# A 32-batch attention and mixture block on one core: projections cut into 64-row half passes that are played between the scores

## The reference, cut to what matters

```
mod = silu(c) @ wmod                                    # six rows per batch: sa, ca, ga, sb, cb, gb
h   = layernorm(x) * (1 + ca) + sa
q, k, v = split(h @ w_qkv.T + b_qkv)
P   = softmax(q @ k.T / 4 + alibi_and_causal_mask)      # per head, 512 x 512
x   = x + ga * ((P @ v) @ w_out.T + b_out)
h   = layernorm(x) * (1 + cb) + sb
p   = softmax(h @ gate_W.T)                             # 8 experts
cnt = [experts of the token with p > 0.3 counted; only the numbers 0 and 1 weigh]
x   = x + gb * ((cnt-weighted sum over two experts) @ out_W.T)
```

## Time and profile before

| | |
|---|---|
| median of 3 runs | 1565.01 us (1564.07 to 1567.11) |
| span of the profiled execution | 1560.2 us, so the runs lie 3.9 to 6.9 us above it (the profiled execution has no time of its own beside its span) |
| PE busy | 1472.0 us, 94% |
| DVE busy | 1277.9 us, 82% |
| ACT busy | 1147.2 us, 74% |
| POOL busy | 858.0 us, 55% |
| mean granted TensorE clock | 0.983 of full speed |

### The profile page before, as it was taken

The page is one execution under the profiler, slowest core; times in us unless marked ns, Lnnn a source line. Parts: engine busy times, 40 slices in busy tenths (PEclk is TensorE's granted clock), DMA queues, the critical chain, the costliest instruction groups (busy, mean ns, idle before and its releaser), DMA issues.

```text
span 1560.2 us, 56229 instructions
## 1 busy us (share of the span) xinstructions
PE 1472.0 (94%) x21476; PEld 946.3 (61%) x21476; DVE 1277.9 (82%) x3030; ACT 1147.2 (74%) x2464; POOL 858.0 (55%) x924
## 2 busy tenths in 40 slices
PE   6888999999999999999999999999999999999996
PEld 5555656666666666666666666656666656666653
DVE  6777888888888888888888888888888888888836
ACT  2477777778777777777877877777777777777762
POOL 2124556556556556655655665565665565566454
PEclk9799999999999999999999999999999999999988
DMA  5344555555455555455555545555545555554521
GB/s 170 99 150 127 171 156 173 152 170 157 149 178 155 175 153 166 143 168 167 157 180 152 160 146 170 166 160 157 165 142 167 175 150 178 154 169 139 157 73 50
DMA packets 197298, 239.73 MB, mean 154 GB/s; under 512 B 22462, under 2 KB 147782, under 8 KB 197030
## 3 DMA queue, kind: packets, MB, share of 16 engines
q1 hardware_dynamic: 196972, 236.07, 49.4%
q10 hardware_dynamic: 64, 0.07, 0.0%
HBM read 134.25 MB, written 100.73 MB: 151 GB/s over the span
## 4 chain that ended last, share of the span: by engine, by line
PE 62%; DVE 10%; DMA 9%; issue 6%; SPq 6%; ACT 3%; POOL 2%; POOLq 0%; DVEq 0%; ACTq 0%
PE ps L599 26%; PE ps L753 11%; PE ps L748 8%; PE ps L807 6%; DMA qk_d<-qk_st 5%; PE ps L802 5%; DVE mxp L1089 3%; DMA kz<-qk_d 2%; PE ps L768 2%; PE ps L662 2%; SPq L412 2%; DVE ve_c L1014 1%; DVE zr L1101 1%; DVE st_c L1000 1%; SPq L429 1%
## 5 line engine op out<-in xcount | busy, mean ns | idle before, releaser
L1089 DVE TENSOR_REDUCE mxp<-ps 128x4 f32<-128x512 f32 (+1 forms) x1536 | 842.8, 592 | 160.5 <-PE ps L768 155.6
L863 ACT ACTIVATE prob<-ps 128x512 f32<-128x512 f32 (+1 forms) x1536 | 732.6, 525 | 121.8 <-PE ps L753 116.4
L753 PE MATMUL ps<-qs,kz 50*128 50x128 f16 (+2 forms) x3584 | 405.9, 240 | 12.9 <-DVE mxp L1089 10.5
L768 PE MATMUL ps<-kz,qs 49*128 49x128 f16 (+1 forms) x4096 | 410.5, 231 | 0.1
L753 PEld LDWEIGHTS ps<-qs,kz 50*128 50x128 f16 x3584 | 261.4, 94 | 88.7 <-ACT prob L863 31.1
L768 PEld LDWEIGHTS ps<-kz,qs 49*128 49x128 f16 x4096 | 286.3, 95 | 3.8 <-DVE mxp L1089 1.8
L1347 POOL TENSOR_TENSOR om<-oc,rz 128x512 f32<-128x512 f32 x62 | 77.4, 1270 | 329.9 <-DMA rz<-rz_d 329.9
L807 PE MATMUL ps<-prob,va 128*32 128x384 f32 (+2 forms) x3072 | 237.6, 381 | 0.0
L748 PE MATMUL ps<-mk 64*128 64x256 bf16 x1024 | 198.6, 274 | 36.0 <-DMA kz<-qk_d 11.3
L802 PE MATMUL ps<-prob,va 128*32 128x128 f32 x4096 | 209.6, 277 | 0.6 <-DVE qk_st L1021 0.6
L764 PE MATMUL ps<-mk 64*128 64x256 bf16 x1024 | 201.0, 276 | 5.4 <-DVE mxp L1089 3.4
(11 more groups left out here) (157 smaller groups left out, 2870.6 us busy)
## 6 DMA issues: line engine op xcount, KB each, us to landing
qk_d<-qk_st SPq DMA_DIRECT2D x128, 256.0 KB, 2.8
ou_d<-ou SPq DMA_DIRECT2D x124, 256.0 KB, 2.3
qs<-qk_d SPq DMA_DIRECT2D x256, 96.0 KB, 2.4
kz<-qk_d SPq DMA_DIRECT2D x256, 96.0 KB, 2.5
xa<-in_L_attn_x SPq DMA_DIRECT2D x32, 512.0 KB, 5.2
qk_d<-qk_st SPq DMA_DIRECT2D x128, 128.0 KB, 3.4
xc<-in_L_attn_x SPq DMA_DIRECT2D x32, 512.0 KB, 4.1
oc<-ou_d SPq DMA_DIRECT2D x31, 512.0 KB, 4.9
```

The costliest lines, as they stand in the source:

```text
L753: x_ = mm(bank[:, col:col + w * P], kz[rows, h // 2, kt * P:(kt + 1) * P], qs[rows, h // 2, qt * P:(qt + w) * P], start=(n > 0), stop=(n > ...
L768: x_ = mm(bank[:, col * P:(col + w) * P], qs[rows, h // 2, qt * P:(qt + 1) * P], kz[rows, h // 2, kt * P:(kt + w) * P], start=(n > 0), sto ...
L863: nc.scalar.activation(prob[:, h % 8, at:at + w], ps[:, ST + n, 0:w], ACT.Exp, scale=1.0 / FS).then_inc(s["exp_done"], 1)
L1089: v.tensor_reduce(mxp[:, g % 2, at, first:first + apart * (BLOCKS[n] - 1) + 1:apart], bank.rearrange("p (m k) -> p m k", k=P), AX.X, ALU.m ...
```

## The change

- All `qk`, `v`, `out` and `moe` products are made in two half passes, one over rows 0 to 63 and one over rows 64 to 127 of the operands, both added up in one PSUM bank. The twelve products of a batch form a ring (`CHAIN`); while product k does its first half pass, product k-1 does its second, matmul by matmul beside it. A half pass is cut in three pieces, and each piece is played in one gap, ahead of that gap's scores: 36 of the 48 gaps of a batch have one.
- These products roll through three banks (4, 5, 6). Bank 7 takes `pv`, `mt`, `ta`, `t2`. Scores and row scores have two banks each, used in turn, and PE waits for the chunk two gaps back.
- `ta`, `t2` and `mt` are transposed in two row halves, the second half behind a wait for the first.
- ACT no longer makes the float16 part of `ta`/`t2` results; POOL copies it from the float32 part. The two small rows of the layernorm leave DVE; POOL makes one of them.
- All tables are new, with one entry per gap. `x1` has two buffers. Offsets are larger: the last expert product and the last sums of a batch fall in the iteration after, and the loop runs to NB + 3.
- The functions for the last two batches, `spread_z` and `TAIL` are gone: the last batches go the way of the others.

```diff
+CHAIN = [("qk", 0, 1, (0, 1, 2)), ("qk", 1, 1, (3, 4, 6)), ("qk", 2, 1, (7, 9, 10)),
+         ("v", 0, 1, (11, 12, 15)), ("qk", 3, 1, (16, 17, 18)), ("v", 1, 1, (20, 23, 24)),
+         ("moe", 0, -2, (26, 27, 28)), ("moe", 1, -2, (29, 30, 31)), ("out", 0, -1, (34, 35, 36)),
+         ("out", 1, -1, (38, 39, 40)), ("moe", 2, -2, (41, 42, 43)), ("moe", 3, -2, (44, 46, 47))]
 PE_AT = {
+    2: [("mt", 1, 0)], 3: [("mt_hi", 1, 0)], 5: [("pv", 3, -1)], 11: [("t2", 0, -2)], 12: [("t2_hi", 0, -2)],
+    14: [("t2", 1, -2), ("t2_hi", 1, -2)], 17: [("mt", 2, 0)], 18: [("mt_hi", 2, 0)], 19: [("pv", 0, 0)],
+    21: [("gate", 0, -2)], 22: [("ta", 0, 2)], 26: [("ta_hi", 0, 2)], 29: [("mt", 3, 0), ("mt_hi", 3, 0)],
+    32: [("pv", 1, 0)], 37: [("ta", 1, 2)], 38: [("ta_hi", 1, 2)], 41: [("mt", 0, 1)], 42: [("mt_hi", 0, 1)],
+    44: [("pv", 2, 0)],
 }
 ACT_AT = {
+    20: [("ou", 0, 0)], 21: [("gate_exp", 0, -2)], 24: [("qk_hi", 3, 1)], 26: [("hf_a", 0, 2)], 29: [("negm", 3, 0)],
+    30: [("oh", 0, -1)], 31: [("oh", 1, -1), ("vst", 1, 1), ("z0", 0, -2)], 32: [("ou", 1, 0)], 36: [("z0", 1, -2)],
...
 SP_AT = {
+    1: [("load_ga", 0, -1)], 8: [("load_aug", 1, 0), ("store_ou", 3, -1)], 9: [("load_o", 0, -1)], 11: [("load_z", 0, -1)],
+    14: [("store_qk", 1, 1)], 16: [("load_c", 0, -1), ("store_qk", 0, 1)], 18: [("store_res", 0, -3)],
+    19: [("load_stack", 0, 1)], 20: [("load_aug", 2, 0), ("load_gb", 0, -2)], 21: [("store_rz", 0, -1), ("store_ou", 0, 0)],
+    22: [("load_a", 0, 3)], 23: [("load_rz", 0, -1), ("store_qk", 2, 1), ("load_stack", 1, 1)], 24: [("store_qk", 3, 1)],
...
+ST, MX = (0, 1), (2, 3)
...
+            def turned(b, n, name, ready, src):
+                dst = to(name, n, b)
+                wait(pe, ready, (b + 1) * QT)
                 for t in range(QT):
+                    x_ = nc.tensor.transpose(dst[:, t * P:t * P + HALF], src[0:HALF, t, n * P:(n + 1) * P], ident[0:HALF, 0:HALF])
+                x_.then_inc(s[f"{name}_half"], 1)
+            def turned_hi(b, n, name, src):
+                wait(pe, f"{name}_half", b * 2 + n + 1)
...
+            def qk(dst, n, j, c, m, u, first, last):
+                rows = slice(HALF * j, HALF * j + HALF)
+                w, h = ((wqkv_hi, hh_a), (wqkv_hi, hl_a), (wqkv_lo, hh_a))[m]
+                col = (n % 2) * D + (n // 2) * P
+                return mm(dst, w[rows, c, col:col + P], h[rows, c, :], start=first, stop=last)
...
+            def chain(i, gap):
...
+                    if live(pb):
+                        wait(pe, "half_done", HALVES[pname, pn, pb])
+                for g in range(2 * place, 2 * place + 2):
+                    for u in range(2):
+                        if live(pb) and u < PIECES[pname]:
+                            x_ = halves[pname][0](ps[:, BANK[pname, pn], :], pn, 1, g // 3, g % 3, u, False, last)
...
+                        if live(b) and u < PIECES[name]:
+                            x_ = halves[name][0](ps[:, BANK[name, n], :], n, 0, g // 3, g % 3, u, (g, u) == (0, 0), False)
...
-                    wait(pe, "exp_done", i * 48 + 3 * t + n - 2)
+                    wait(pe, "exp_done", i * 48 + 3 * t + n - 1)
-                    wait(pe, "mx_read", bm * 48 + 3 * pos + n - 2)
+                    wait(pe, "mx_read", bm * 48 + 3 * pos + n - 1)
```

More of the change, by code:

```diff
@@ L110 @@
 HALF = 64
+PIECES = {"qk": 1, "v": 2, "out": 2, "moe": 1}
+ST, MX = (0, 1), (2, 3)
 PARTS = 48
@@ L311, in bank_of, with iterations, play @@
-        def bank_of(name, n, b):
-            return TAIL[name, n, b][0] if (name, n, b) in TAIL else MISC + BANK[name, n]
         def live(b):
             return 0 <= b < NB
-        def iterations(eng, one, drain=None, end=0):
-            for i in range(-2, NB + end if drain else NB + 2):
+        def iterations(one):
+            for i in range(-2, NB + 3):
                 one(i)
-            if drain:
-                drain()
         early = ("load_a", "bn_a", "ag_a", "norm_a")
-        def play(i, t, table, steps, part=None, late={}):
-            for place in range(4):
-                for at, name, n, off in table.get(t, []):
-                    if at == place and live(i + off) and not (name in early and i + off == 0):
+        def play(i, table, steps, part=None, late={}):
+            for gap in range(GAPS):
+                for name, n, off in table.get(gap, []):
+                    if live(i + off) and not (name in early and i + off == 0):
@@ L331, in play @@
                         steps[name](i + off, n)
-                    elif at == place and i + off == -2 and (name, n) in late:
+                    elif i + off == -2 and (name, n) in late:
                         late[name, n]()
-                if part is not None and place < 3:
-                    part(i, t, place)
-        SIDE = [(t, name, n, off) for t in range(SLOTS) for at, name, n, off in sorted(PE_AT.get(t, []), key=lambda x: x[0])]
+                if part is not None:
+                    part(i, gap)
@@ L339, in before @@
+        HIGH = ("ta_hi", "t2_hi", "mt_hi")
+        SIDE = [x[1:] for x in sorted([(gap, name, n, off) for gap in PE_AT for name, n, off in PE_AT[gap] if name not in HIGH]
+                                      + [(gaps[0] + 0.5, name, n, off) for name, n, off, gaps in CHAIN], key=lambda x: x[0])]
         def before(name, n, b):
[L341 to L342 removed]
+            at = [k for k, x in enumerate(SIDE) if x[0:2] == (name, n)][0]
+            i = b - SIDE[at][2]
@@ L350, in before @@
             return None
+        HALVES = {}
+        for i in range(-2, NB + 3):
+            for name, n, off, _ in CHAIN:
+                if live(i + off):
+                    HALVES[name, n, i + off] = len(HALVES) + 1
         def max_at(i, t):
@@ L538, in one @@
             def one(i):
-                for t in range(SLOTS):
-                    play(i, t, SP_END if i == PRE else SP_AT, steps)
-            iterations(sp, one, drain, -1)
-            wait(sp, "res_stored", (NB + 1) * 16)
+                play(i, SP_AT, steps)
+            iterations(one)
+            wait(sp, "res_stored", NB * 16)
         @block.tensor
@@ L1308, in _, with largest @@
-            iterations(dve, one, drain)
+                def largest(i, gap):
+                    bm, pos = max_at(i, gap // 3)
+                    if live(bm):
+                        maxima(bm, pos, gap % 3)
+                play(i, DVE_AT, steps, largest, late)
+            iterations(one)
         @block.gpsimd
```

650 lines of the change are left out of this document (172 added, 478 removed), and 13 rows, old and new, of the table PE_AT.

## The result

The changed kernel takes 1790.8 us (median; 1784.0 to 1795.0) against 1566.1 us: the ratio is 1.143, with a 95% interval of 1.139 to 1.146. It is slower by 14%, and above the range of the prediction.

A forecast was written before the change was run, and what follows sets the result against it. PE's order of work was taken to bound the kernel; -2.0 + 2.2 + 0.5 + 0.2 + 0.3 = +1.2 us a batch, +38 us over 32 batches, plus 17 for the end, gave 1620 us; range 1510 to 1690.

The forecast's parts named there:

- DMAs: Stack loads at gap 24 and `oh` at gap 30: no difference, bounds -0.6 and +2 us a batch.
- POOL: Four added copies, up to 4.7 us on 27.1 of 45.8 us a batch, would be hidden by POOL's idle time.
- Two banks: Score banks: PE runs one gap ahead instead of two, +0.3 us a batch, bounds -0.7 and +3.
- Rival 2: Two banks make DVE and ACT the pace: +3 us a batch, 1706 us; chance 0.15 together with Rival 4.
- The slack that I gave ACT and DVE: Dropped float16 reads and small rows: ACT loses 3.1, DVE some 1.6 us a batch; neither sets the batch.
- Transpositions: `ta`, `t2`, `mt` in halves: each costs what a whole does, bound by weight load, +2.2 us a batch; lower bound 0.
- Rival 1: Transpositions not bound by the load and DMA waits go: -2.0 us a batch, 1518 us; chance 0.26.
- Excursions: PE's switches between 64-row scores and 128-row work: 13 of 18 go at 0.15 us each, -2.0 us a batch.
- half passes side by side: Products on PE: paired half passes stream together, six pairs again take 6 x 0.2155 us, no loss.
- Rival 4: Pieces don't run side by side: 1.55 us a batch per tenth lost, 1670 us for one; chance 0.15 with Rival 2.
- The end: After the last score: longer sums' passage, POOL products and extra half passes, +17 us, bounds +8 and +25.
- The start: Before the first score: the order is kept, so 0 us.

The follow-up runs named there:

- a_order: Changed kernel with the store of q/k part 0 issued ahead of the load of the sums, load of c and result store moved to gap 20: 1774.9 us (1.133).
- c_sp2: Changed kernel with the queue order putting the sums' path first, next input loaded before c, gains and result store; POOL's subtraction kept: 1716.9 us (1.094).
- c_sp2_xn: c_sp2 with POOL adding a negated mean in place of subtracting the mean: 1607.7 us (1.028).
- a_xn: Changed kernel with POOL making a negated mean once a batch and adding it, in place of subtracting the mean: 1793.1 us (1.143).
- b_two: Kernel before with two of three banks used in turn for each kind of score, waiting for the release two moves back: 2014.5 us (1.286).
- a_ox_full: a_order_xn with whole 128-row transpositions in place of the row halves, issued where the first half stood: 1827.6 us (1.166).
- c_sp2_full: c_sp2_xn with whole 128-row transpositions in place of the row halves, at the place of the first half: 1626.4 us (1.039).
- a_order_xn: a_order with POOL adding a negated mean in place of subtracting the mean: 1800.2 us (1.151).

## Why the prediction was wrong, point by point

**The step that failed** is "DMAs": "I take no difference, bounds -0.6 and +2". It named both places (the second `qk` store behind `load_c`, and `oh` at gap 30 with a margin of 20.8 against 19 us) and then priced the sum of them at nothing. Together they cost 3.6 + 2.0 us of ACT's time a batch, and PE's idle time rose by 4.9 us. Four errors are in it. The two waits add up, since they are eleven gaps apart, and the first alone is beyond the bound. PE's stall behind the first is in a place that I hadn't named, the product bank that `v` 1 needs from `qk` 2 (3.1 us), and not the stack at gap 24. The passage of the sums was taken at its old 20.8 us, but SP's new order made it 24.9. And the slow clock behind each idle stretch was in no term. A clock of 0.93 on two levels means a seventh of the time at the lower one, 7 us a batch; since PE doesn't have to be the pace in it, at most half of that is lost. How much it is exactly, no run here isolates.

**POOL** "hidden by its idle time" failed as well. I counted four copies (measured 0.61 us each, 2.4 and not 4.7 us) and did not count the changed operation in a line that looked like the old one. The idle time is real (37% of the span) but not where the block stands: behind it queue `hh_c`, `hl_c` and the copy of the values, for which PE and ACT wait in `a_order` and `c_sp2`, and the result, for whose store the queue engine waits in the changed kernel. In the best order the price is 109 us (`c_sp2` against `c_sp2_xn`), 3.4 us a batch; in the changed kernel itself it is hidden behind the other stalls (`a_xn`, no difference). Either failure alone leaves the time outside the range: 1717 us with the queue repaired (`c_sp2`), 1793 with POOL repaired (`a_xn`); only both repairs reach it.

**Two banks**, +0.3 with bounds of -0.7 and +3: in `c_sp2_xn` PE waits (27.0 + 13.3) / 24 = 1.7 us a batch for maxima and exponentials, for 0.7 before. +1.0 us, inside the bounds. Rival 2 as stated (+3 a batch) doesn't hold; but two banks in the order of before cost 13.9 us (`b_two`), so the smallness of this term hangs on the new order, by what the traces show on the pieces between the chunks. The slack that I gave ACT and DVE (3.1 and 1.6 us a batch) doesn't show in their busy time: 35.1 and 40.5 us a batch in `c_sp2_xn`, for 35.7 and 38.9. That two banks also turn any wait of ACT over a gap into PE's is argued; no run has this order with three. (My 34 us outside the `pv` should have been 45.8 - 9.2 = 36.6.)

**Transpositions**, +2.2: too high, the lower bound of 0 was right. Halves are 0.06 us apart, so two cost what a whole one does, and they run beside the scores. Whole ones cost 27 and 19 us more (`a_ox_full`, `c_sp2_full`), about what their eight excursions cost by the prices above. The nearest row, a 128-row load with 32 moving columns, wasn't near: half the rows made the difference. Rival 1 had this part right.

**Excursions**, -2.0, and half passes side by side: right as far as they can be read. The pairs are 0.22 us apart and the scores join at once. (The six whole matmuls of before are (730.35 - 729.26) / 5 = 0.218 us apart on average, 0.2155 only behind the first; it changes nothing in the sum.) In `c_sp2_xn` PE is busy for 1031.56 / 1100 x 46.4 = 43.5 us a batch, for 44.3 before, -0.8 with the added waits of pieces and the clock of 0.99 in it; the single term isn't isolated. Rival 4 is refuted.

**The end**, +17 with bounds of 8 and 25: measured +29. PE runs much of it at half clock (0.50 from 1720 to 1740 and from 1750 to 1770 us), which was in no term, and among the last four sums DVE waits 4.3 and 5.1 us for ACT's `z`. In `c_sp2_xn` it is +24. **The start**, 0: measured +13, +10 in `c_sp2_xn`. The first `qk` eviction comes at 29.25 us for 22.39, so half of it is there before the first projection is out. POOL's fast form took 2.6 us off it in one order (62.2 us in `a_order_xn`, 64.8 in `a_order`) and added 2.0 in another (67.3 in `a_xn`, 65.3 in the changed kernel); the cause stays open.

**The sum**: the range held the repaired kernel (1608 us for 1620 predicted), not the one that was built, and partly by cancelling errors. `c_sp2_xn` is 2.4 to 3.1% slower than before, and in its profiled execution (the longest of the six) that consists of the end (24 us), the start (10 us) and 0.6 us a batch. No version here beats the kernel before.

## What to carry to other kernels

When a schedule is rewritten, follow each loop that crosses engines through every queue it passes, with lengths from the trace, and compare it with the gaps that the schedule allows; where two margins are within 2 us, price them as stalls that add up and not as one doubtful term. A repair that changes nothing isn't refuted: several stalls in one batch cover each other, and a repair shows its worth only when the others are made too (POOL's operation alone +2 us, the queue order alone -74, the two together -183). Read the operation in a changed line as closely as the place of the line.

## What the runs showed of the hardware that was not expected

- POOL's `tensor_scalar` of 128x256 float32 with subtract and multiply takes 1222 ns, with add and multiply 559 ns. The operand's place doesn't matter (1223 ns for the subtraction from a tile of its own).
- Float32 transpositions of 64 rows with 64 moving columns start about 0.06 us apart beside 64-row scores; whole ones (128 by 128) are 0.11 us apart.
- The queue engine's waits stand in front of everything behind them. The Trainium skill has this in DMA: Bandwidth & Descriptors (Anatomy of one DMA — SWDGE (gpsimd) path): an engine of the DMA never waits for a semaphore, the sequencer that issues does. The trace agrees: the reciprocals lay ready for 6.1 us (751.38 to 757.46) while transfers before them in the order were waited for.
